# Rounded three-pass down products in a four-layer transformer block, with the low parts subtracted on VectorE

## The reference

```python
x = x + _L0_xattn_ref(_layernorm(x), ctx, ctx, mask, ...)     # 16 heads
x = x + _L0_ffn_ref(_layernorm(x), ...)                       # 8 experts, 512 hidden, top 2
x = x + _L1_xattn_ref(_layernorm(x), ctx, ...)                # self, then cross, then feed-forward
x = x + _L1_ffn_ref(_layernorm(x), ...)                       # 32 experts, 64 hidden, top 6, and a shared one

# _L0_ffn_ref
h = gelu(einsum('td,edh->eth', xf, W1) + b1[:, None, :])
expert_out = einsum('eth,ehd->etd', h, W2) + b2[:, None, :]
out = einsum('etd,te->td', expert_out, weights)

# _L1_ffn_ref, one expert
g, u = xf @ gu[:I].T, xf @ gu[I:].T
acc = acc + c[:, None] * (silu(g) * u @ dn.T)
```

## Time and profile before

| | before |
|---|---|
| median of 3 runs | 594.29 us (592.61 to 595.97) |
| the profiled execution | 594.72 us |
| its span, first to last instruction | 592.9 us |
| mean granted TensorE clock | 0.994 |
| TensorE busy | 566.6 us, 96% |
| VectorE busy | 399.4 us, 67% |
| ScalarE busy | 323.7 us, 55% |
| GpSimd busy | 104.6 us, 18% |
| DMA queues | 20% of their time in use |

### The profile page before, as it was taken

One profiled execution on the slowest core, in us unless ns is written; L12 is line 12 of the kernel. 1 busy time (PEld: TensorE's weight loads), 2 busy tenths in 40 slices (PEclk: granted clock), 3 DMA queues, 4 the chain that ended last, 5 costly groups with the idle time before them and its releaser, 6 DMA issues.

```text
span 592.9 us, 8098 instructions
## 1 busy us (share of the span) xinstructions
PE 566.6 (96%) x2512; PEld 372.9 (63%) x2512; DVE 399.4 (67%) x1265; ACT 323.7 (55%) x566; POOL 104.6 (18%) x120
## 2 busy tenths in 40 slices
PE   2799999999999999999999999999899999999997
PEld 2666667665666666656676567565667766676664
DVE  4889899783212444648557675778889899677564
ACT  1478687867445466844775458854385342343221
POOL 3102020000211210242122315235200011100000
PEclk9899999999999999999999999999899999999999
DMA  2601000030211120111101021053211332342441
GB/s 78 233 19 28 1 10 2 2 143 19 58 49 36 38 71 19 35 38 36 36 35 36 2 64 36 20 175 112 89 72 53 112 109 87 113 141 67 134 138 40
DMA packets 23306, 38.35 MB, mean 65 GB/s; under 512 B 3776, under 2 KB 9536, under 8 KB 22880
## 3 DMA queue, kind: packets, MB, share of 16 engines
q1 hardware_dynamic: 22832, 37.44, 19.9%
q10 hardware_dynamic: 432, 0.40, 0.3%
HBM read 36.45 MB, written 1.38 MB: 64 GB/s over the span
## 4 chain that ended last, share of the span: by engine, by line
PE 84%; DVE 7%; ACT 4%; issue 3%; DMA 1%; POOL 1%; ACTq 0%; DVEq 0%
PE ps L1682 17%; PE ps L1493 10%; PE ps L1495 9%; PE ps L1494 9%; PE ps L1852 9%; PE ps L1569 4%; PE ps L1488 4%; PE ps L1589 3%; PE ps L1500 2%; PE ps L1604 2%; PE ps L1601 2%; PE ps L1759 2%; PE ps L1739 1%; PE ps L1749 1%; DVE NM L1156 1%
## 5 line engine op out<-in xcount | busy, mean ns | idle before, releaser
L1493 PE MATMUL ps<-xThi,w1s 128*128 128x512 f32 x256 | 144.4, 564 | 2.1 <-DVE h L1445 2.1
L911 ACT ACTIVATE h<-ps,early 128x512 f32<-128x512 f32 x128 | 86.8, 687 | 79.5 <-PE ps L1495 65.7
L1682 PE MATMUL ps<-h,w2s 128*128 128x512 f32 x256 | 122.1, 594 | 0.2 <-DVE ty L1245 0.2
L1495 PE MATMUL ps<-xTlo,w1s 128*128 128x512 f32 x256 | 101.4, 396 | 0.0
L1494 PE MATMUL ps<-xThi,w1s 128*128 128x512 f32 x256 | 100.8, 394 | 0.0
L1002 ACT ACTIVATE s<-ps 128x512 f32<-128x512 f32 x68 | 40.7, 599 | 101.2 <-PE ps L1495 100.9
L1493 PEld LDWEIGHTS ps<-xThi,w1s 128*128 128x128 f32 x256 | 48.6, 190 | 36.5 <-issue 16.9
L1682 PEld LDWEIGHTS ps<-h,w2s 128*128 128x128 f32 x256 | 46.7, 189 | 33.4 <-issue 24.1
L1445 DVE TENSOR_TENSOR h<-s,ps 128x512 f32<-128x512 f32 x68 | 46.5, 684 | 28.7 <-PE ps L1495 25.8
L1494 PEld LDWEIGHTS ps<-xThi,w1s 128*128 128x128 f32 x256 | 48.8, 190 | 25.9 <-issue 21.4
L1852 PE MATMUL ps<-h,w2s 128*128 128x512 f32 x128 | 64.2, 594 | 0.9 <-DVE h L1451 0.9
(11 more groups left out here) (264 smaller groups left out, 884.8 us busy)
## 6 DMA issues: line engine op xcount, KB each, us to landing
CB<-ct_rows SPq DMA_DIRECT2D x128, 128.0 KB, 2.9
WB<-wt_rows SPq DMA_DIRECT2D x32, 256.0 KB, 3.2
w2s<-w_dram SPq DMA_DIRECT2D x2, 2048.0 KB, 8.1
raw<-gu_dram SPq DMA_DIRECT2D x4, 512.0 KB, 5.5
x_in<-x_dram SPq DMA_DIRECT2D x4, 256.0 KB, 2.8
w2s<-dn_dram SPq DMA_DIRECT2D x1, 1024.0 KB, 7.2
...
```

Source lines behind the costliest of these rows:

```text
L911: nc.scalar.activation(h32[:, c % HR, :], bank[c % 2], ACT.Gelu, bias=b1T[:, c:c + 1]).then_inc(b_gelu.sem, 1)
L1493: M(dst, w[0], xThi[:, x, :], start=start, stop=False)
L1495: return M(dst, w[0], xTlo[:, x, :], start=False, stop=stop)
L1682: M(bank[2], w2s[:, c * P:(c + 1) * P], h32[:, c % HR, :], start=(c % 4 == 0), stop=(c % 4 == 3)).then_inc(b_y.sem, 1)
```

## The change

The down products of the odd chunks of stage B (64 of 128) and all of stage D (68) no longer are one float32 matmul. They are three passes of float32r, `down3`: high weights by high data, low weights by high data, high weights by low data. Even chunks of stage B stay as they were.

For the data this adds, for each of the 132 products, a rounding copy on ScalarE (`highs_b`, `highs_d`) and a subtraction on VectorE (`lows_b`, `lows_d`). The high part goes to `hh0`, which shares its memory with `s32`, or to `hh1`, which shares it with `WB`; the low part is written over `h32` itself. For the weights it adds roundings on ScalarE and subtractions on GpSimd: `split2` makes those of stage B (two pieces of 128x1024, each 8 chunks of 128), `split3` those of stage D (one of 128x128 and four of 128x512). `split3` can't begin its four large pieces before the last down product of stage B, since `w2h` holds the high weights of stage B until then. The planner's tables are new throughout. With THREE = 0 the branch `b < THREE` is never taken.

```diff
--- before.py
+++ after.py
@@ -97,6 +97,10 @@
     def at(self, b, k):
...
+    def followed(self, b, per):
+        return Signal(self.sem, per, self.at(b, 0))
...
     def sig(name, per):
         return Signal(ctx.enter_context(nc.semaphore(name)), per)
+    def twins(name, shape):
+        with nc.sbuf_tensor(name, shape, F32) as plain:
+            pass
+        return plain, sb(name + "_r", shape, F32R)
...
     xTlo = sb("xTlo", [P, 2, S], F32R)
-    h32 = sb("h32", [P, 4, S])
+    h32, h32r = twins("h32", [P, 4, S])
...
     w1s = sb("w1s", [P, 2, NC0 * P], F32R)
-    w2s = sb("w2s", [P, NC0 * P])
+    w2s, w2r = twins("w2s", [P, NC0 * P])
     w1raw = w2s
-    gus, dns = w1s, w2s[:, 0:NP1 * P]
+    w2h = sb("w2h", [P, NP1 * P], F32R)
+    odd, odd_low = (w.rearrange("p (c two k) -> p c two k", two=2, k=P)[:, :, 1, :] for w in (w2s[:], w2r[:]))
+    gus, dns, dn_low = w1s, w2s[:, 0:NP1 * P], w2r[:, NP1 * P:]
     shs = sb("shs", [P, 2, 2 * P], F32R)
     shd = sb("shd", [P, P])
+    shh = sb("shh", [P, 2, P], F32R)
...
+    WB, hh1 = twins("WB", [P, 2, S])
+    s32, hh0 = twins("s32", [P, 2, S])
...
     b_h_ps, b_gelu, b_y = (sig(n, NC0) for n in ("b_h_ps", "b_gelu", "b_y"))
+    b_hi, b_lo = a_oz.followed(NB, NC0 // 2), a_on.followed(NB, NC0 // 2)
...
     d_g_ps, d_u_ps, d_silu, d_t, d_dn = (sig(n, ND) for n in ("d_g_ps", "d_u_ps", "d_silu", "d_t", "d_dn"))
+    d_hi, d_lo = b_hi.followed(NB, ND), b_lo.followed(NB, ND)
...
+    THREE = 0
+    NDN = 1 + 4
+    w2_hi, w2_lo = Signal(w1_hi.sem, 0, NHALF), Signal(zeros.sem, 0, NZERO)
+    dn_hi, dn_lo = Signal(w1_hi.sem, 0, NHALF + 2), Signal(zeros.sem, 0, NZERO + 2)
+    def down1_piece(k):
+        c = slice(512 * (k - 1), 512 * k)
+        return (dns[:, c], w2h[:, c], dn_low[:, c]) if k else (shd[:], shh[:, 0, :], shh[:, 1, :])
...
 PLAN_ACT = {
...
+    "split2": [[13379, 15321]],
...
 PLAN_DVE = {
...
+    "lows_b": [[14225, 14285, 14601, 15095, 15244, 15754, 15878, 16317, 16489, 17096, 17347, 17483, 17982, 18293,
...
+        def split2():
+            for k in range(2):
+                yield
+                pool.wait_ge(w2_hi.sem, w2_hi.at(0, k + 1))
+                o, c = slice(8 * k, 8 * k + 8), slice(1024 * k, 1024 * k + 1024)
+                nc.gpsimd.tensor_tensor(odd_low[:, o, :], odd[:, o, :], w2h[:, c].bitcast(F32).rearrange("p (c k) -> p c k", k=P),
+                                        ALU.subtract).then_inc(w2_lo.sem, 1)
+        def split3():
+            for k in range(NDN):
+                yield
+                pool.wait_ge(dn_hi.sem, dn_hi.at(0, k + 1))
+                w, hi, low = down1_piece(k)
+                nc.gpsimd.tensor_tensor(low, w, hi.bitcast(F32), ALU.subtract).then_inc(dn_lo.sem, 1)
...
+        def split2():
+            for k in range(2):
+                yield
+                act.wait_ge(down0_loaded.sem, 16)
+                c = slice(1024 * k, 1024 * k + 1024)
+                copy(w2h[:, c].rearrange("p (c k) -> p c k", k=P), odd[:, 8 * k:8 * k + 8, :]).then_inc(w2_hi.sem, 1)
+        def split3():
+            for k in range(NDN):
+                yield
+                w, hi, _ = down1_piece(k)
+                act.wait_ge(down1_loaded.sem, 32)
+                if k:
+                    act.wait_ge(b_y.sem, b_y.at(NB - 1, NC0))
+                copy(hi, w).then_inc(dn_hi.sem, 1)
+        def highs_b(b):
+            for j in range(NC0 // 2):
+                yield
+                act.wait_ge(b_gelu.sem, b_gelu.at(b, 2 * j + 2))
+                if b or j >= 2:
+                    act.wait_ge(b_y.sem, b_y.at(b, 2 * j - 2))
+                copy(hh0[:, j % 2, :], h32[:, (2 * j + 1) % HR, :]).then_inc(b_hi.sem, 1)
+        def highs_d(b):
+            for n in range(ND):
+                yield
+                t = b * ND + n
+                if n:
+                    act.wait_ge(d_h.sem, d_h.at(b, n))
+                else:
+                    act.wait_ge(d_t.sem, d_t.at(b, 1))
+                if b == THREE and n < 2:
+                    act.wait_ge(b_ty.sem, b_ty.at(NB - 1, E0))
+                if b > THREE or n >= 2:
+                    act.wait_ge(d_dn.sem, d_dn.at(b, n - 1))
+                copy(hh1[:, t % 2, :], h32[:, t % HR, :]).then_inc(d_hi.sem, 1)
...
                 if b * ND + n >= 2:
                     act.wait_ge(d_t.sem, d_t.at(b, n - 1))
+                else:
+                    act.wait_ge(b_y.sem, b_y.at(NB, 0))
...
                ("prepare_b", map(prepare_b, every)), ("base", map(base, every)), ("gelus", map(gelus, every)),
-               ("split1", [split1()]), ("stage_c", map(stage_c, every)), ("exps_c", map(exps_c, every)),
+               ("split1", [split1()]), ("split2", [split2()]), ("split3", [split3()]), ("highs_b", map(highs_b, every)),
+               ("highs_d", map(highs_d, every[THREE:])), ("stage_c", map(stage_c, every)), ("exps_c", map(exps_c, every)),
...
+        def lows_b(b):
+            for j in range(NC0 // 2):
+                yield
+                dve.wait_ge(b_hi.sem, b_hi.at(b, j + 1))
+                o = (2 * j + 1) % HR
+                V.tensor_tensor(h32r[:, o, :], h32[:, o, :], hh0[:, j % 2, :].bitcast(F32), ALU.subtract).then_inc(b_lo.sem, 1)
+        def lows_d(b):
+            for n in range(ND):
+                yield
+                t = b * ND + n
+                dve.wait_ge(d_hi.sem, d_hi.at(b - THREE, n + 1))
+                V.tensor_tensor(h32r[:, t % HR, :], h32[:, t % HR, :], hh1[:, t % 2, :].bitcast(F32), ALU.subtract).then_inc(d_lo.sem, 1)
...
+        def down3(dst, w, x, start, stop):
+            (whi, wlo), (xhi, xlo) = w, x
+            M(dst, whi, xhi, start=start, stop=False)
+            M(dst, wlo, xhi, start=False, stop=False)
+            return M(dst, whi, xlo, start=False, stop=stop)
...
                     pe.wait_ge(down0_loaded.sem, 16)
-                pe.wait_ge(b_gelu.sem, b_gelu.at(b, c + 1))
-                M(bank[2], w2s[:, c * P:(c + 1) * P], h32[:, c % HR, :], start=(c % 4 == 0), stop=(c % 4 == 3)).then_inc(b_y.sem, 1)
+                j, at, ends = c // 2, c % 4 == 0, c % 4 == 3
+                if c % 2:
+                    pe.wait_ge(b_lo.sem, b_lo.at(b, j + 1))
+                    if b == 0 and j % 8 == 0:
+                        pe.wait_ge(w2_lo.sem, w2_lo.at(0, j // 8 + 1))
+                    w = w2h[:, j * P:(j + 1) * P], odd_low[:, j, :]
+                    down3(bank[2], w, (hh0[:, j % 2, :], h32r[:, c % HR, :]), at, ends).then_inc(b_y.sem, 1)
+                else:
+                    pe.wait_ge(b_gelu.sem, b_gelu.at(b, c + 1))
+                    M(bank[2], w2s[:, c * P:(c + 1) * P], h32[:, c % HR, :], start=at, stop=ends).then_inc(b_y.sem, 1)
...
             for n in range(ND):
                 yield
-                if n:
-                    pe.wait_ge(d_h.sem, d_h.at(b, n))
+                if n == 0:
+                    claim(2)
+                c, t = slice((n - 1) * P, n * P), b * ND + n
+                if b < THREE:
+                    if n:
+                        pe.wait_ge(d_h.sem, d_h.at(b, n))
+                    else:
+                        pe.wait_ge(d_t.sem, d_t.at(b, 1))
+                        if b == 0:
+                            pe.wait_ge(down1_loaded.sem, 32)
+                    w = dns[:, c] if n else shd[:]
+                    M(bank[2], w, h32[:, t % HR, :], start=(n == 0), stop=(n == ND - 1)).then_inc(d_dn.sem, 1)
                 else:
-                    claim(2)
-                    if b == 0:
-                        pe.wait_ge(down1_loaded.sem, 32)
-                    pe.wait_ge(d_t.sem, d_t.at(b, 1))
-                w = shd[:] if n == 0 else dns[:, (n - 1) * P:n * P]
-                M(bank[2], w, h32[:, (b * ND + n) % HR, :], start=(n == 0), stop=(n == ND - 1)).then_inc(d_dn.sem, 1)
+                    if b == THREE and (n == 0 or n % 4 == 1):
+                        pe.wait_ge(dn_lo.sem, dn_lo.at(0, 1 + (n + 3) // 4))
+                    pe.wait_ge(d_lo.sem, d_lo.at(b - THREE, n + 1))
+                    w = (w2h[:, c], dn_low[:, c]) if n else (shh[:, 0, :], shh[:, 1, :])
+                    down3(bank[2], w, (hh1[:, t % 2, :], h32r[:, t % HR, :]), n == 0, n == ND - 1).then_inc(d_dn.sem, 1)
```

More of the change, by code:

```diff
@@ L132 @@
[L132 to L136 removed]
+    "constants": [[0, 15, 32, 60, 289, 838, 866]],
+    "norm_a": [[710, 737], [1760, 1787], [4158, 4185], [7297, 7325]],
@@ L137 @@
+    "split2": [[13480, 15423]],
+    "split3": [[38309, 39191, 40595, 40722, 40848]],
+    "stage_c": [[19407, 19434, 22703, 22730, 24237, 24264, 25236, 26302, 26329], [25935, 25962, 29170, 29198, 30609,
+        30636, 32630, 32970, 32997], [32499, 32526, 35766, 35793, 37532, 37559, 38053, 39063, 39090], [39318, 39345,
+        43111, 43138, 45229, 45256, 46414, 47778, 47805]],
+    "norm_d": [[28442, 29738], [35047, 35894], [42367, 42394], [49938, 49965]],
 }
@@ new lines @@
+    "halves_b": [[11652, 13086], [16615, 17205], [24068, 24586], [27639, 28279]],
```

(26 more changed lines are left out.)

224 lines of the change are left out of this document (104 added, 120 removed), and 195 rows, old and new, of tables (PLAN_ACT, PLAN_DVE, PLAN_PE, PLAN_SP).

## The result

| | kernel before | changed kernel |
|---|---|---|
| median | 594.51 us (592.61 to 595.97, 4 runs) | 602.45 us (601.78 to 604.93, 4 runs) |
| ratio, 95% interval | | 1.014 (1.012 to 1.016) |
| profiled execution, span | 592.9 us | 600.0 us |
| until the first gate product | 140.3 | 137.2 |
| stage B | 267.5 | 271.6 |

The change makes the kernel 1.4% slower: +7.1 us in the spans, where +1.2 was forecast. The first two stages are bounded by the first gate product of the first layer and the first VectorE product of stage D; then comes the first VectorE product of the last batch. That last one stands at 549.70 in the kernel before, not at 551.9, as the prediction had it from the earlier trace rows, and so its three batches take 141.9 us, not 144.1 (the second batch, too, ends at 508.3 and not at 511.4).

A forecast was written before the change was run, and what follows sets the result against it. TensorE was taken to bound the kernel, with VectorE becoming the bound in stage D's first three batches. Stage B -8.4, those batches +11.6 and the last -2.0 sum to +1.2, forecast 595.5 us, range 587.5 to 603.5.

The forecast's parts named there:

- its term: Stage B: 10.9 us saved by three passes less 2.5 of stalls, -8.4 us.
- the prediction's own signs: Whole kernel: wrong if D's first three batches stay below 148 us, stage B shows many subtraction waits, or clock below 0.95.
- No cheaper: Rival, changed down products: three passes save nothing, taking away 10.9 + 3.1 us, 609.5 us; chance 0.03.
- +11.6: Stage D, first three batches: +2.6 as VectorE becomes the bound, +7.5 held by GpSimd, +1.5 waiting for TensorE.
- VectorE's own need, 146.7: Stage D, first three batches: VectorE's 117.4 us less one product (0.7) plus 50 subtractions at 0.60.
- forecast 7.5: Stage D, first three batches: time GpSimd's pieces hold VectorE up, the middle of 4.2 and 10.4 us.
- -2.0 forecast: Last batch of stage D: -3.1 us from shorter steps, +1.1 behind the last gate.
- I take 2.5: Stage B: new stalls of TensorE on the changed products, between none and 5 us.
- Two instructions among these were only held up: Stage D, first three batches, kernel before: VectorE's L406 and L1352 lost 4.2 us beside GpSimd's subtraction L748.
- The chain's arithmetic: Stage B: gelu, copy, subtraction, down product take 2.7 us against 5.9 of four buffers, so it closes with little left.
- The rival of the clock: TensorE's waits for VectorE in D's first three batches lower its clock, +6 us, 601.5 us; chance 0.23.
- VectorE keeps up: Rival: GpSimd holds VectorE no more than 4.2 us in D, stage B loses nothing, 588 us; chance 0.27.

The follow-up runs named there:

- e4: Changed kernel with GpSimd made quiet (additions to acc_o on 32 of 512 columns, low parts of weights written as zeros): 583.18 us.
- e2: Changed kernel with three passes in stage D alone, stage B's down products plain, new tables of order: 602.15 us.
- e3: Changed kernel with no three-pass down products, only the new tables of order: 595.38 us.
- c2: Changed kernel with GpSimd's sums and low parts of weights moved to VectorE, three passes only in stage B and the last batch: 588.00 us.
- c4: All down products plain in the new order, with GpSimd's sums and low parts of weights moved to VectorE: 592.06 us.
- e5: Kernel before with GpSimd made quiet (additions to acc_o on 32 of 512 columns, low parts of weights written as zeros): 587.49 us.

## Why the prediction was right and wrong

**Right:** slower had the largest chance of the three, if by little, and 602.45 lies in the range (587.5 to 603.5), near its upper end; the forecast itself, 595.5, was 7 too low. That it was not further off is luck: stage B came out 12.5 us worse than its term, the three batches 4.4 better, and the 3.2 us that the new order gained ahead of stage B stood nowhere in the sum. By the prediction's own signs it failed in stage B, which shows many waits on the subtraction (26, with 21.3 us, some of them weight loads that TensorE's matmuls hide). Three terms hold.

- A changed product's three passes come 0.23 us apart. "No cheaper" is out.
- VectorE becomes the bound of D's first three batches. +11.6 became +7.2, and the term that was too large is VectorE's own need, 146.7. With GpSimd quiet (e4, the three batches) it is 138.5:

```profile
397.37:538.30 140.93, 134.59 (x614) 99.42 (x614) 138.52 (x406) 89.92 (x157) 15.82 (x21) 1.00 0.31 94
```

  Held up 147.2 - 138.5 = 8.7, forecast 7.5 (added up in the changed kernel's own trace: 9.6 in eight instructions); idle 1.9, forecast 1.5. The prediction took two held instructions in the kernel before; a third, L403 at 408.41 with 0.96 us, it passed over. Subtractions of over 1 us beside GpSimd's pieces came as forecast, the longest with 2.37. The three batches of e2, and then of e3:

```profile
407.49:558.12 150.63, 137.85 (x615) 100.72 (x614) 147.14 (x406) 90.37 (x157) 24.94 (x21) 0.99 0.27 86
405.58:549.48 143.90, 140.16 (x565) 91.87 (x564) 117.59 (x357) 60.80 (x104) 17.95 (x17) 1.00 0.30 92
```

  The price of a subtraction was right. Held time left out, the 50 of them add 30.3 us to VectorE's busy time, 0.61 each. What they were added to was too high, 116.7 us: the other instructions take 115.8 in the kernel before, 111.6 in e3 in the new order, and 107.1 in the changed kernel, with none gone but one product. By the earlier trace rows a product behind an independent instruction adds 0.60 and one after a gap its full 0.69; in a fuller queue fewer of them stand after a gap.
- The last batch: -2.0 forecast, -1.1 measured to VectorE's last instruction. The step is 2.07 us near the end (VectorE's first product at 585.10 and 587.17), 2.08 forecast, against 2.25 in the earlier trace rows. Others take 2.41, so that the steps give 2.4 us instead of 3.1; what follows the last of them grew by 1.2, forecast 1.1.

**Wrong: stage B's stalls.** The step that failed is "I take 2.5, as TensorE's stalls in this stretch are only 1.8 us now". Stage B was to go from 268 to 259 and went to 271.6. From e3's 268.7 three passes should lead to 257.8; the missing 13.8 us stand where 2.5 were taken and 5 was the upper end. Two thirds of them can be read from TensorE's trace (its busy time shows 8.4 of them as idle, since an instruction that is held after it began counts as busy): the time from the end of the instruction before to its own end, summed over the 64 changed products, is 53.2 us, 0.83 each, so that three passes cost nearly what one plain product does (0.87 in the kernel before). At 0.69 each they would be 44.2, so 9.0 us of the loss stand at these products. In e4 they take 0.72 each, in c2 0.75. Of the 13.8, quieting GpSimd gives back 10.9. What is left, 2.9, is near the 2.5 that I had taken. But a kernel with plain products gains from it too: c4, which has GpSimd's sums moved, is 2.2 below e3. So about 8.7 belong to the three passes and GpSimd together; this is an estimate, as c4's GpSimd work is moved and not taken away.

I had the mechanism, and used it in stage D alone: "Two instructions among these were only held up". In stage B GpSimd was busy 70 us, mostly with 1.28 us additions, and held VectorE there too, for 11.0 us. Before, that cost stage B 1.8 us (267.5 to 265.7 in e5), as TensorE waited for little of it. I read the small cost as a small risk. The chain's arithmetic, 2.7 us in a ring of 5.9, took each link at its median, and the link on VectorE is whatever stands ahead of it in the queue: one held instruction adds up to 2 us.

The Trainium skill (SBUF — State Buffer, Who interferes with whom) says that a VectorE instruction with two SBUF inputs contends with a GpSimd instruction that reads SBUF. The traces agree: 2.34 us for a 128x4 step beside one of 2.38. The same section of the Trainium skill lists `tensor_scalar` among those that can contend, on conditions, and L453 agrees too, 2.55 us for two. I had counted the two-input ones alone.

**The rival of the clock** is not the cause. TensorE waited 3.73 us in the first batch, and the passes behind it came at full rate (TensorE over time):

```profile
432.01 0.50 PE L1620 MATMUL ps<-xThi,w1s 128*128 128x512 f32 x1 [3.73 <-DVE h L1571]
432.36 0.40 PE L1621 MATMUL ps<-xThi,w1s 128*128 128x512 f32 x1
432.59 0.39 PE L1622 MATMUL ps<-xTlo,w1s 128*128 128x512 f32 x1
```

The granted clock was 1.00 in all four batches and 0.99 in stage B, where it fell once, at 399.5 us, behind the two waits of 1.92; the kernel before has one such fall too, at 426.1. Both profiled executions have a mean of 0.994 and differ by 7.1 us. The three other runs of the changed kernel had 0.984 to 0.989 and took 602.3 to 604.9 us, so some 0.7 us of its median may be the clock's. The time came out where this rival had it, 601.5, for another reason. *VectorE keeps up* is out: it needed stage B to lose nothing, and GpSimd to hold VectorE no more than 4.2 us in the three batches.

**Not settled.** Even with GpSimd quiet, stage B saves 5.8 us of the 10.9 against c4. 2.0 of that are waits on the changed products themselves; the rest I did not trace to one cause.
